# Chunked delta rule: three pairs of small matrix products issued alternately on the tensor engine, and the outputs of a tile computed half a step later

## The chip, the cores and the metric

One core of one Trainium2 chip runs the whole program as one launch. The metric is the device time of the program in microseconds (us), lower is better. An engine is named as the profile names it: PE (TensorE matrix products), PEld (its weight loads), DVE (VectorE), ACT (ScalarE), POOL (GpSimd). Each engine takes its instructions strictly in the order in which they are written; semaphores order the engines against each other.

## The reference, cut to what matters

The program is a two-layer decoder over x of 64 x 64 x 128. The change lies in one stage, the gated delta rule of the second layer, which the reference writes as a scan over 64 time steps:

```python
def step(carry, ins):
    s, mem = carry
    ...
    alpha = jnp.where(active > 0, alpha, jnp.ones_like(alpha))
    beta = beta * active
    s = s * alpha[..., None]
    pred = jnp.einsum('bhk,bhkv->bhv', kt, s)
    s = s + (beta * kt)[..., None] * (vt - pred)[:, :, None, :]
    out = jnp.einsum('bhk,bhkv->bhv', qt, s)
    return ((s, mem), out)
...
y = y * jax.lax.rsqrt(jnp.mean(y * y, axis=-1, keepdims=True) + EPS) * head_norm_w
y = y.reshape(B, T, H * dv)
gate = jax.nn.sigmoid(jax.nn.silu(x @ Wu1 + bu1) @ Wu2 + bu2)
y = x + y @ Wo * gate
```

All else (attention, cross attention, two mixtures, layer norms) is the same in both kernels.

## The kernel before, in words

The stage is `delta_rule`. The 64 sequences are cut into NT = 32 tiles of two sequences (TT = 128 tokens); a tile holds HB = 8 pairs of heads and sequences, and two heads share the 128 partitions, so that every small product is one of 64 x 64 on one half of the partitions. In place of the scan, a 64-step triangular system is solved by doubling: six levels (0 to 5) of decayed products of keys and queries (`level_one`), and beside them the inverse G and its transpose GT, grown level by level.

Two kinds of small product exist. `stay` takes its inputs from a half of the partitions and writes to the same half; `cross` writes to the other half. Each issues two products, one for each half, and an fp32 product is two matmul instructions in the trace. One block of eight `stay` (or eight `cross`) is 32 matmuls. Two of the blocks were already issued alternately, one `stay`, one `cross`: `z_and_level` (level l+1 and the step z of the inverse, 64 matmuls, from line 1895) and `g_and_gt` (the growth of G and of GT, 64 matmuls, from line 1916; at the top level, 4, only GT, 32 matmuls).

The work runs in a software pipeline by hand. `half(w_, x, y)` is one step of it: tile x goes through its levels, tile y = x + 1 is prepared (projections, gates, norms, values, `diagonal`, `level_zero`), and tile w_ = x - 1 is finished. `half` is written out for each engine, and the order of the calls in it is the order of that engine's queue. A tile is finished on PE by: `read_v` (GT times v, `cross`), `corrected` (the correction CT times RV, `cross`), `solve` (GT times W, `cross`), `outputs` (U times PT, `stay`), `head_norm`, `project_out`; each was a block of its own. `level_zero` (32 matmuls, `stay`) and `diagonal` were two more. Beside them ACT copies results out of PSUM (`keep_z`, `keep_rv`, `keep_u`, `square_y`) and does logarithms and exponentials; DVE scales, masks and adds (`scale`, `keep_ct`, `keep_pt`, `add_g`, `add_gt`, `subtract`, `strengths`, `normalise_y`); POOL scales the keys (`scale`), starts G and GT (`begin_g`, `begin_gt`), and does `push_logits`, `pair` and `floor_y`. After the last tile, `end` finishes tile 31.

PE's order in a half before: z_and_level 0, project_gates, read_v, g_and_gt 0, beta_sums, project_kq (first half), z_and_level 1, corrected, g_and_gt 1, count, project_kq (second half), z_and_level 2, solve, g_and_gt 2, outputs, norms, z_and_level 3, values, head_norm, g_and_gt 3, level_zero, diagonal, z_and_level 4, project_out, g_and_gt 4.

Of the kernel before, what the change touches and what calls it, by code (L numbers as in the profile page):

```python
# [14 lines left out]
ALU = mybir.AluOpType  # L15
# [1679 lines left out]
def delta_rule(k, s, w, hT, uT, gate, signs, yT):  # L1695
# [19 lines left out]
    log_q, q_eps = s.sb("log_q", [P, HB * T]), two("q_eps", [P, HB * T])  # L1715
# [3 lines left out]
    ylog, yinv = flat(RV), flat(W)  # L1719
# [56 lines left out]
    def in_turn(eng, front, half, end):  # L1776

        front(0)
        half(None, 0, 1)
        for tile in range(NT - 2):  # L1780
            half(tile, tile + 1, tile + 2)
        half(NT - 2, NT - 1, None)
        end(NT - 1)

    @block.tensor
    def _(pe):
# [67 lines left out]
        def norms(w_, y):  # L1854

            if w_ is not None:
                pe.wait_ge(u_kept, upto(w_))
# [23 lines left out]

        def level_zero(y):

            pe.wait_ge(kq_ready, upto(y))
            for n in range(HB):
                last = level_one(y, 0, n, F2)
            last.then_inc(level_ready[0], 1)
# [45 lines left out]
        def read_v(w_):  # L1933

            u = par(w_)
            pe.wait_ge(gt_kept[TOP], upto(w_))
            pe.wait_ge(out_kept, upto(w_))
            for n in range(HB):
                last = cross(lambda r: E0[r, wide(n)], lambda r: GT[u][r, n, :], lambda r: v[u][r, n % 2, n // 2, :])
            last.then_inc(rv_ready, 1)  # L1940

        def corrected(w_, y):
# [4 lines left out]
            pe.wait_ge(rv_kept, upto(w_))  # L1947
            pe.wait_ge(ct_kept[LEVELS - 1], upto(w_))
            for n in range(HB):
                last = cross(lambda r: E1[r, wide(n)], lambda r: CT[LEVELS - 1][r, n, :], lambda r: RV[r, n, :])  # L1950
            last.then_inc(crv_ready, 1)

        def solve(w_):

            u = par(w_)
            pe.wait_ge(w_ready, upto(w_))
            for n in range(HB):
                last = cross(lambda r: E0[r, wide(n)], lambda r: GT[u][r, n, :], lambda r: W[r, n, :])
            last.then_inc(u_ready, 1)

        def outputs(w_):

            u = par(w_)
            pe.wait_ge(u_kept, upto(w_))
            pe.wait_ge(pt_kept[LEVELS - 1], upto(w_))
            for n in range(HB):
                last = stay(lambda r: E1[r, wide(n)], lambda r: U[r, n, :], lambda r: PT[u][r, n, :])
            last.then_inc(y_ready, 1)

        def head_norm(w_, y):  # L1970

            u = par(w_)
            if y is not None:
                pe.wait_ge(logn_ready, upto(y))
            pe.wait_ge(floored, upto(w_))
# [10 lines left out]
        def front(y):  # L1986
# [4 lines left out]
            norms(None, y)  # L1991
            values(y)
            diagonal(y)
            level_zero(y)

        def end(w_):
            read_v(w_)
            corrected(w_, None)
            solve(w_)
            outputs(w_)  # L2000
            head_norm(w_, None)
            project_out(w_)

        def half(w_, x, y):
            z_and_level(w_, x, 0)
            if y is not None:
                project_gates(y, range(DP))
            if w_ is not None:
                read_v(w_)
            g_and_gt(w_, x, 0)  # L2010
            if y is not None:
                beta_sums(y)
                project_kq(y, (0, 1))
            z_and_level(w_, x, 1)
            if w_ is not None:
                corrected(w_, y)
            g_and_gt(w_, x, 1)
            if y is not None:
                count(y)
                project_kq(y, (2, 3))  # L2020
            z_and_level(w_, x, 2)
            if w_ is not None:
                solve(w_)
            g_and_gt(w_, x, 2)
            if w_ is not None:
                outputs(w_)
            if y is not None:
                norms(w_, y)
            z_and_level(w_, x, 3)
            if y is not None:  # L2030
                values(y)
            if w_ is not None:
                head_norm(w_, y)
            g_and_gt(w_, x, 3)
            if y is not None:
                level_zero(y)
                diagonal(y)
            z_and_level(w_, x, 4)
            if w_ is not None:
                project_out(w_)  # L2040
            g_and_gt(w_, x, 4)

        in_turn(pe, front, half, end)

    @block.scalar
    def _(act):
# [45 lines left out]
        def query_eps(w_, y):  # L2092
# [4 lines left out]
            if w_ is not None:  # L2097
                act.wait_ge(floored, upto(w_))
            act.activation(q_eps[par(y)][:, :], log_q[:, :], ACT.Square, scale=RMS_EPS ** 0.5, bias=q_floor[:, :]
# [16 lines left out]
        def square_y(w_):  # L2116
            act.wait_ge(y_ready, upto(w_))
            act.activation(ysq[:, :], E1, ACT.Square).then_inc(ysq_ready, 1)  # L2118
# [22 lines left out]
        def end(w_):  # L2141
            keep_rv(w_)
            keep_u(w_)
            square_y(w_)
            log_y(w_)
            inverse_y(w_)

        def half(w_, x, y):
            keep_z(x, 0)
            if y is not None:  # L2150
                stage(y)
            if w_ is not None:
                keep_rv(w_)
            keep_z(x, 1)
# [3 lines left out]
            keep_z(x, 2)  # L2158
            if w_ is not None:
                keep_u(w_)  # L2160
            if y is not None:
                square(y)
            if w_ is not None:
                square_y(w_)
            if y is not None:
                log_norms(y)
                log_queries(y)
                exp_beta(y)
            keep_z(x, 3)
            if y is not None:  # L2170
                exp_norms(y)
                query_eps(w_, y)
            if w_ is not None:
                log_y(w_)
                inverse_y(w_)
            keep_z(x, 4)

        in_turn(act, front, half, end)

    @block.gpsimd  # L2180
    def _(pool):
# [31 lines left out]
        def floor_y(w_):  # L2213
# [3 lines left out]
            pool.tensor_tensor(ysq[:, :], ysq[:, :], q_eps[par(w_)][:, :], ALU.add).then_inc(floored, 1)  # L2217
# [26 lines left out]
        def end(w_):  # L2244
            floor_y(w_)

        def half(w_, x, y):
            if y is not None:
                push_logits(y)
            scale(x, 1)  # L2250
            scale(x, 2)
            scale(x, 3)
            if w_ is not None:
                floor_y(w_)
            if y is not None:
                pair(y)
            scale(x, 4)
            if y is not None:
                begin_gt(w_, y)
                scale(y, 0)  # L2260
                begin_g(y)
# [3 lines left out]
        in_turn(pool, front, half, end)  # L2265

    @block.vector
    def _(dve):
# [75 lines left out]
        def diagonal(w_, y):  # L2344

            dve.wait_ge(diag_ready, upto(y))
            if w_ is not None:
                dve.wait_ge(y_ready, upto(w_))
# [84 lines left out]
        def front(y):  # L2433
# [7 lines left out]
            diagonal(None, y)  # L2441
# [3 lines left out]
            keep_pt(y, 0)  # L2445

        def end(w_):
            subtract(w_)
            normalise_y(w_)
            keep_out(w_)  # L2450

        def half(w_, x, y):
            keep_ct(x, 1)
            if y is not None:
                stage(y)
            decays(x, 1)
            keep_pt(x, 1)
            scale(x, 1)
            add_g(x, 0)
            if y is not None:  # L2460
                beta_logits(y)
                raise_logits(y)
# [698 lines left out]
```

## Time and profile before

| what | us |
|---|---|
| median of 3 runs | 2336.43 (2326.97 to 2350.22) |
| the profiled execution | 2313.16 |
| its span on the core | 2311.4 |
| PE busy in the span | 2062.0 (89%) |
| DVE busy | 1504.5 (65%) |
| ACT busy | 1108.9 (48%) |
| POOL busy | 686.6 (30%) |

The profile is one execution, and lies 1% below the median of the runs. A matmul's end is modelled in it, so the distance from the start of one block to the start of the next tells more than the duration of a block. The loop of the delta rule lies between 1059 and 1943 us of the span.

### The profile page before, as it was taken

To read this page: it belongs to the slowest core of one execution; us is meant where nothing else is said; L and a number is where in the kernel's file an instruction comes from. 1 tells how busy PE (TensorE), PEld (TensorE's weight loads), DVE (VectorE), ACT (ScalarE), POOL (GpSimd) and SP (SyncE) were. 2 spreads that over 40 slices of the span, in tenths; PEclk is the share of its full clock that TensorE was granted. 3 is DMA by queue.
4 is the path that set the end of the run, shared out by engine and by line. 5 is a ranking of instruction groups with operands and counts; after the bars stand their busy time and mean duration, and the time that the engine had idled before them with its cause. 6 is when DMAs were issued, how large, how long until landed. Compare 5 with 4: busy or idle time off the path is not lost. (4 is left out here: it accounts for less than half of the span.)

```text
span 2311.4 us, 90647 instructions
## 1 busy us (share of the span) xinstructions
PE 2062.0 (89%) x39947; PEld 1450.0 (63%) x39947; DVE 1504.5 (65%) x3187; ACT 1108.9 (48%) x1883; POOL 686.6 (30%) x731
## 2 busy tenths in 40 slices
PE   6999999789986779687999999999999996997998
PEld 3566666555643568126877888888787884445445
DVE  7878787456657744586777777777777774354214
ACT  2233334556667775673545444455454443244334
POOL 4656565022204100303333333333333332000000
PEclk7999999999998999898999999999999997997999
DMA  4000000000000000100000000000000001002001
GB/s 94 2 2 2 3 2 2 6 1 0 0 3 12 0 1 1 31 0 3 5 4 5 4 4 5 4 4 5 4 4 4 4 4 52 0 1 73 1 0 37
DMA packets 36492, 22.62 MB, mean 10 GB/s; under 512 B 16809, under 2 KB 32113, under 8 KB 36146
## 3 DMA queue, kind: packets, MB, share of 16 engines
q1 hardware_dynamic: 36146, 17.38, 3.0%
q8 instruction: 294, 4.82, 0.9%
q14 instruction: 52, 0.43, 0.1%
HBM read 15.28 MB, written 2.10 MB: 8 GB/s over the span
## 5 line engine op out<-in xcount | busy, mean ns | idle before, releaser
L1793 PEld LDWEIGHTS psum<-dr_kq,dr_kSq 64*64 64x64 f32 x6144 | 196.3, 134 | 64.1 <-issue 55.2
L1793 PE MATMUL psum<-dr_kq,dr_kSq 64*64 64x64 f32 x6144 | 222.2, 221 | 7.6 <-DVE dr_G L2404 2.9
L2105 ACT ACTIVATE dr_Y<-psum 128x256 f32<-128x256 f32 x160 | 62.9, 393 | 311.1 <-PE psum L1799 309.5
L1793 PE MATMUL psum<-dr_GT,dr_Y 64*64 64x32 f32 x5120 | 187.0, 221 | 12.7 <-issue 12.0
L1799 PE MATMUL psum<-dr_G,dr_CT 64*64 64x32 f32 x5120 | 184.1, 221 | 0.4 <-issue 0.2
L1793 PEld LDWEIGHTS psum<-dr_GT,dr_Y 64*64 64x64 f32 x5120 | 166.2, 135 | 19.0 <-issue 14.6
L1799 PEld LDWEIGHTS psum<-dr_G,dr_CT 64*64 64x64 f32 x5120 | 165.0, 134 | 1.0 <-issue 0.8
L2194 POOL TENSOR_TENSOR dr_kSq<-dr_kSq,dr_decay 128x256 f32<-128x256 f32 x128 | 99.4, 777 | 211.1 <-PE psum L1793 208.1
L1799 PE MATMUL psum<-dr_Y,dr_GT 64*64 64x32 f32 x4096 | 147.4, 219 | 14.6 <-issue 13.4
L1799 PEld LDWEIGHTS psum<-dr_Y,dr_GT 64*64 64x64 f32 x4096 | 135.3, 135 | 39.8 <-issue 37.8
L2395 DVE COPY_PREDICATED dr_PT<-dr_level_masks,psum 128x256 f32<-128x256 uint32 x192 | 102.7, 535 | 83.5 <-PE psum L1793 80.6
L2385 DVE TENSOR_TENSOR dr_CT<-psum,dr_minus_masks 128x256 f32<-128x256 f32 x192 | 78.5, 422 | 77.5 <-PE psum L1793 77.5
L2370 DVE TENSOR_TENSOR dr_kq<-dr_kq,dr_decay 128x512 f32<-128x512 f32 x128 | 114.5, 895 | 0.0
L537 ACT ACTIVATE attn_probsT<-psum 128x1024 f32<-128x1024 f32 x32 | 32.7, 1023 | 165.3 <-PE psum L383 165.3
L503 POOL TENSOR_TENSOR attn_q<-attn_by_cos,attn_by_sin 128x512 f32<-128x512 f32 x64 | 81.3, 1270 | 72.2 <-DVE attn_by_sin L450 71.0
L503 POOL TENSOR_TENSOR attn_k<-attn_by_cos,attn_by_sin 128x512 f32<-128x512 f32 x64 | 81.4, 1271 | 70.9 <-DVE attn_by_sin L450 70.3
L2217 POOL TENSOR_TENSOR dr_ysq<-dr_ysq,dr_q_eps 128x512 f32<-128x512 f32 x32 | 40.5, 1266 | 138.3 <-ACT dr_ysq L2118 138.3
L2413 DVE TENSOR_TENSOR dr_GT<-dr_GT,psum 128x256 f32<-128x256 f32 x160 | 66.3, 415 | 16.1 <-PE psum L1793 16.1
L3004 DVE COPY topk_outs<-psum 128x512 f32<-128x512 f32 x16 | 11.1, 692 | 99.9 <-PE psum L2894 99.9
L2202 POOL TENSOR_TENSOR dr_push<-dr_spikes_t,dr_alpha_spike 128x512 f32<-128x512 bf16 x32 | 37.9, 1185 | 118.1 <-ACT dr_spikes_t L2053 118.1
L2404 DVE TENSOR_TENSOR dr_G<-dr_G,psum 128x256 f32<-128x256 f32 x128 | 53.2, 416 | 27.1 <-PE psum L1799 25.9
L450 DVE SCALAR_TENSOR_TENSOR attn_by_cos<-psum,attn_qk_bias,attn_rope_q 128x512 f32<-128x512 f32 x64 | 47.8, 747 | 33.3 <-PE psum L356 32.2
(396 smaller groups left out, 5655.1 us busy)
## 6 DMA issues: line engine op xcount, KB each, us to landing
topk_w<-in_L_ffn_w_dram SPq DMA_DIRECT2D x16, 256.0 KB, 5.9
attn_w_x_rows<-in_x_dram SPq DMA_DIRECT2D x4, 512.0 KB, 6.0
out_dram<-store_rows SPq DMA_DIRECT2D x4, 512.0 KB, 4.0
dout_w<-in_L_attn_Wff_dram SPq DMA_DIRECT2D x3, 256.0 KB, 2.9
attn_w_rows<-in_L_attn_Wq_dram SPq DMA_DIRECT2D x1, 256.0 KB, 6.7
attn_w_rows<-in_L_attn_Wk_dram SPq DMA_DIRECT2D x1, 256.0 KB, 6.1
attn_w_rows<-in_L_attn_Wv_dram SPq DMA_DIRECT2D x1, 256.0 KB, 5.5
attn_w_rows<-in_L_attn_Wo_dram SPq DMA_DIRECT2D x1, 256.0 KB, 4.9
```

Source lines behind the costliest of these rows:

```text
L450: last = dve.scalar_tensor_tensor(dst[:, :].rearrange("p (n t) -> p n t", t=T), k.bank[2 * r + part][:, :].rearrange("p (n t) -> p n t", t=T),
L503: pool.tensor_tensor(qk[st % 2][g][:, hp, :], by_cos[st % 2][:, :], by_sin[st % 2][:, :], ALU.add).then_inc(roped, 1)
L1793: last = nc.tensor.matmul(out(r), lhsT(r), rhs(r), start=True, stop=True)
L1799: last = nc.tensor.matmul(out(HALVES[1 - j]), lhsT(r), rhs(r), start=True, stop=True)
L2105: act.activation(half_of(Y[l], l, 0), ZG[:, ZS].rearrange("p (m l) -> p m l", l=1 << l), ACT.Copy).then_inc(z_kept[l], 1)
L2194: pool.tensor_tensor(ks, ks, total.unsqueeze(2).to_broadcast([P, HB * (LR >> l), 1 << l]), ALU.mult).then_inc(kS_scaled[l], 1)
L2217: pool.tensor_tensor(ysq[:, :], ysq[:, :], q_eps[par(w_)][:, :], ALU.add).then_inc(floored, 1)
L2370: dve.tensor_tensor(right, right, pair[:, :, 0].unsqueeze(1).unsqueeze(3).to_broadcast([P, 2, HB * (LR >> l), L]), ALU.mult).then_inc(scal ...
L2385: dve.tensor_tensor(right4(CT[l], l), out[:, 0, :, :, :], minus.to_broadcast(shape), ALU.mult).then_inc(ct_kept[l], 1)
L2395: dve.copy_predicated(right4(PT[u], l), mask.bitcast(U32).to_broadcast(shape), out[:, 1, :, :, :]).then_inc(pt_kept[l], 1)
L2404: dve.tensor_tensor(left, left, ZG[:, RS].rearrange("p (m l) -> p m l", l=1 << l), ALU.add).then_inc(g_kept[l], 1)
L2413: dve.tensor_tensor(right, right, GTB[:, ZS].rearrange("p (m l) -> p m l", l=1 << l), ALU.add).then_inc(gt_kept[l], 1)
```

## The change

Three pairs of PE blocks become one block each, in which a `stay` and a `cross` alternate, as in `z_and_level`: `read_and_output(o, w_)` (the value read of tile w_ with the outputs of tile o = w_ - 1), `correct_and_level(w_, y)` (the correction of w_ with level zero of y), and `solve_and_gt(o, w_, x, y)` (the solve of w_ with the growth of GT at the top level of x). The outputs of a tile are now computed in the next half, so a half spans four tiles, `half(o, w_, x, y)`, and there is one more half; `end` is gone. The order of the calls changes on all four engines; `q_eps` gets a third buffer, and the logarithm of the head norm goes to `ysq` in place of `RV`. No instruction of computation is added or dropped.

```diff
-    log_q, q_eps = s.sb("log_q", [P, HB * T]), two("q_eps", [P, HB * T])
+    log_q, q_eps = s.sb("log_q", [P, HB * T]), [s.sb(f"q_eps{u}", [P, HB * T]) for u in range(3)]
...
-    ylog, yinv = flat(RV), flat(W)
+    ylog, yinv = ysq[:, :], flat(W)
...
+        def read_and_output(o, w_):
+
+            if w_ is not None:
+                pe.wait_ge(gt_kept[TOP], upto(w_))
+            if o is not None:
+                pe.wait_ge(u_kept, upto(o))
+                pe.wait_ge(pt_kept[LEVELS - 1], upto(o))
             for n in range(HB):
...
+                    last_v = cross(lambda r: E0[r, wide(n)], lambda r: g[r, n, :], lambda r: values_of[r, n % 2, n // 2, :])
+                if o is not None:
+                    last_y = stay(lambda r: E1[r, wide(n)], lambda r: U[r, n, :], lambda r: PT[par(o)][r, n, :])
...
+        def correct_and_level(w_, y):
...
+                pe.wait_ge(kq_ready, upto(y))
...
+                pe.wait_ge(rv_kept, upto(w_))
+                pe.wait_ge(ct_kept[LEVELS - 1], upto(w_))
             for n in range(HB):
...
+                    last_level = level_one(y, 0, n, F2)
...
+                    last = cross(lambda r: E1[r, wide(n)], lambda r: CT[LEVELS - 1][r, n, :], lambda r: RV[r, n, :])
...
+        def solve_and_gt(o, w_, x, y):
...
+                pe.wait_ge(w_ready, upto(w_))
...
+                pe.wait_ge(z_kept[TOP], upto(x))
+                pe.wait_ge(gt_kept[TOP - 1], upto(x))
...
```

The four queues of a full half after the change:

- PE: z_and_level 0, read_and_output, project_gates, g_and_gt 0, head_norm(o), z_and_level 1, project_kq (first half), count, g_and_gt 1, project_kq (second half), z_and_level 2, project_out(o), beta_sums, g_and_gt 2, norms, z_and_level 3, g_and_gt 3, correct_and_level, z_and_level 4, values, solve_and_gt, diagonal.
- ACT: stage(y), keep_z 0, square_y(o), keep_rv(w_), log_y(o), inverse_y(o), keep_z 1, gate(y), keep_kSq(y), keep_z 2, square(y), exp_beta(y), keep_z 3, log_norms, log_queries, exp_norms, keep_z 4, query_eps(y), keep_u(w_).
- POOL: push_logits(y), floor_y(o), scale 1, scale 2, scale 3, pair(y), scale 4, begin_g(y), scale(y, 0), begin_gt(y).
- DVE: scale 1, diagonal, keep_pt 0 and 1, keep_ct 1, add_g 0, stage(y), decays 1, raise_logits(y), add_gt 0, keep_pt 2, scale 2, keep_ct 2, add_g 1, decays 2, normalise_y(o), add_gt 1, gates(y), keep_pt 3, keep_out(o), scale 3, keep_ct 3, add_g 2, beta_logits(y), weigh(y), add_gt 2, decays 3, keep_pt 4, scale 4, keep_ct 4, add_g 3, add_gt 3, strengths(y), subtract(w_), scale(y, 0), keep_pt 5, keep_ct(y, 0), keep_ct 5, add_gt 4, decays(y, 0), keep_v(y).

## Rows read from the trace of the kernel before

**Rows 1.** The page: busy time by engine, and PE clock in 40 slices.

```profile
PE 2062.0 (89%) x39947; PEld 1450.0 (63%) x39947; DVE 1504.5 (65%) x3187; ACT 1108.9 (48%) x1883; POOL 686.6 (30%) x731
...
PEclk7999999999998999898999999999999997997999
```

**Rows 2.** Busy time by stretch: length, then PE, PEld, DVE, ACT, POOL, clock, DMA.

```profile
1103.75:1918.42 814.67, 775.38 (x25456) 657.12 (x25460) 611.90 (x1616) 398.32 (x655) 299.31 (x299) 1.00 0.02 4
```

**Rows 3.** Source line L2118: count, ns min/median/max, first and last start.

```profile
L2118 ACT ACTIVATE dr_ysq<-psum x31: 597/597/597, 1103.7 to 1918.4; 128x512 f32<-128x512 f32 x31
```

**Rows 4.** PE's waits, 1100 to 1930: line, releaser, us in total, times, longest.

```profile
PE psum L1793 <- issue: 17.4, 24, 1.2
PE psum L1799 <- issue: 16.8, 24, 1.2
PE psum L1793 <- DVE dr_G L2404: 2.9, 3, 1.6
```

**Rows 5.** PE's timeline from 1501.8: start, us, then [idle before].

```profile
1501.86 1.07 PE L1799 MATMUL psum<-dr_RV,dr_CT 64*64 64x64 f32 x30
1502.72 0.25 PE L1793 MATMUL psum<-dr_GT,dr_Y 64*64 64x32 f32 x2
...
1503.43 0.25 PE L1793 MATMUL psum<-dr_GT,dr_Y 64*64 64x32 f32 x2 [0.23 <-issue]
...
1506.93 0.24 PE L1799 MATMUL psum<-dr_G,dr_CT 64*64 64x32 f32 x1
...
1510.68 0.32 PE L1793 MATMUL psum<-dr_PT,dr_U 64*64 64x64 f32 x2 [0.72 <-issue]
1510.94 1.08 PE L1860 MATMUL psum<-dr_head_sum,dr_sq 128*128 128x32 f32 x8
...
1512.89 0.27 PE L1793 MATMUL psum<-dr_kq,dr_kSq 64*64 64x64 f32 x2
...
1513.96 1.08 PE L1871 MATMUL psum<-dr_wv,dr_h 128*64 128x256 f32 x8
1514.98 1.13 PE L1976 MATMUL psum<-dr_ysq,dr_head_mean 128*128 128x512 f32 x2
1516.03 0.25 PE L1799 MATMUL psum<-dr_Y,dr_GT 64*64 64x32 f32 x2
...
1517.00 1.13 PE L1793 MATMUL psum<-dr_kq,dr_kSq 64*64 64x64 f32 x32
```

**Rows 6.** PE's timeline, another run of pauses.

```profile
1611.31 0.25 PE L1799 MATMUL psum<-dr_Y,dr_GT 64*64 64x32 f32 x2 [0.45 <-issue]
...
1618.69 0.53 PE L1860 MATMUL psum<-dr_head_sum,dr_sq 128*128 128x32 f32 x4 [0.45 <-issue]
```

**Rows 7.** DMA, 1103.75 to 1918.42: queue, packets, MB, share.

```profile
q8 instruction: 202, 3.31, 1.7%
```

**Rows 8.** DMA, 1501 to 1511, in 40 slices of 0.25 us: busy tenths.

```profile
DMA  2000000000000020000000000000300000000000
```

**Rows 9.** DVE, by shape, 1100 to 1930, and its timeline around `strengths`.

```profile
L2370 DVE TENSOR_TENSOR dr_kq<-dr_kq,dr_decay 128x512 f32<-128x512 f32 x122 | 109.3, 896 | 0.0
...
L2395 DVE COPY_PREDICATED dr_PT<-dr_level_masks,psum 128x256 f32<-128x256 uint32 x183 | 97.6, 533 | 79.4 <-PE psum L1793 76.5
...
1515.67 0.69 DVE L2318 TENSOR_SCALAR dr_length<-dr_norm 64x4 f32<-64x4 f32 x4
...
1517.76 0.42 DVE L2404 TENSOR_TENSOR dr_G<-dr_G,psum 128x256 f32<-128x256 f32 x1
```

**Rows 10.** The page: ACT's `keep_z` and POOL's `floor_y`; xcount, busy, mean ns, idle before.

```profile
L2105 ACT ACTIVATE dr_Y<-psum 128x256 f32<-128x256 f32 x160 | 62.9, 393 | 311.1 <-PE psum L1799 309.5
...
L2217 POOL TENSOR_TENSOR dr_ysq<-dr_ysq,dr_q_eps 128x512 f32<-128x512 f32 x32 | 40.5, 1266 | 138.3 <-ACT dr_ysq L2118 138.3
```

**Rows 11.** The last tile after the loop: ACT's and DVE's timeline.

```profile
1928.67 0.60 ACT L2110 ACTIVATE dr_RV<-psum 128x512 f32<-128x512 f32 x1 [3.66 <-PE psum L1799]
...
1942.61 0.29 DVE L2431 TENSOR_TENSOR delta_hT<-psum,ctx_rows 128x128 f32<-128x128 f32 x1 [2.17 <-PE psum L1982]
```

More of the change, by code:

```diff
@@ L1953, in solve @@
[L1953 to L1968, printed above, removed]
@@ L1990, in front, with half @@
             count(y)
-            norms(None, y)
+            norms(None, None, y)
             values(y)
             diagonal(y)
[L1994 to L2005, printed above, removed]
+            correct_and_level(None, y)
+        def half(o, w_, x, y):
+            if x is not None:
+                z_and_level(w_, x, 0)
+            read_and_output(o, w_)
@@ L2021, in half @@
[L2021 to L2029, printed above, removed]
+            if x is not None:
+                g_and_gt(w_, x, 2)
+            if y is not None:
+                norms(o, w_, y)
+            if x is not None:
+                z_and_level(w_, x, 3)
+                g_and_gt(w_, x, 3)
@@ L2444, in front, with half @@
             scale(y, 0)
[L2445 to L2453, printed above, removed]
+        def half(o, w_, x, y):
+            if x is not None:
+                scale(x, 1)
+                diagonal(o, x)
+                keep_pt(x, 0)
+                keep_pt(x, 1)
+                keep_ct(x, 1)
+                add_g(x, 0)
             if y is not None:
                 stage(y)
[L2456 to L2459, printed above, removed]
+            if x is not None:
+                decays(x, 1)
+            if y is not None:
+                raise_logits(y)
+            if x is not None:
+                add_gt(x, 0)
+                keep_pt(x, 2)
+                scale(x, 2)
+                keep_ct(x, 2)
+                add_g(x, 1)
+                decays(x, 2)
+            if o is not None:
+                normalise_y(o)
+            if x is not None:
+                add_gt(x, 1)
+            if y is not None:
+                gates(y)
+            if x is not None:
+                keep_pt(x, 3)
+            if o is not None:
+                keep_out(o)
+            if x is not None:
+                scale(x, 3)
+                keep_ct(x, 3)
+                add_g(x, 2)
@@ L2460, in half @@
             if y is not None:
                 beta_logits(y)
-                raise_logits(y)
-            add_gt(x, 0)
-            keep_pt(x, 2)
-            scale(x, 2)
+                weigh(y)
+            if x is not None:
+                add_gt(x, 2)
+                decays(x, 3)
+                keep_pt(x, 4)
+                scale(x, 4)
+                keep_ct(x, 4)
+                add_g(x, 3)
+                add_gt(x, 3)
+            if y is not None:
+                strengths(y)
@@ L2505, in _ @@
-        in_turn(dve, front, half, end)
+            if x is not None:
+                keep_ct(x, 5)
+                add_gt(x, 4)
+            if y is not None:
+                decays(y, 0)
+                keep_v(y)
+        in_turn(front, half)
 def delta_output(k, yT):
```

225 lines of the change are left out of this document (105 added, 120 removed).

## The prediction

> **What bounds the kernel now.** I read the page first, then the timeline of one tile on every engine, then the waits of PE, then the DMA queues. PE is busy 89% of the span and 95% of the delta loop: 775.38 of 814.67 us, at a granted clock of 1.00, that is 2.4 GHz [rows 1, 2]. The squares of the outputs come once a tile; the 31 of them from 1103.7 to 1918.4 enclose 30 periods, so a tile takes 814.67 / 30 = 27.16 us [rows 2, 3]. DVE, next in the list, works 611.90 / 30 = 20.4 us of it [rows 2]. In the timeline one PE block starts where the one before ends; PE waits for data almost nowhere: of its idle time by releaser, 34.2 us are "issue" and 2.9 us a DVE result [rows 4]. "Issue" is time in which the profile shows nothing to wait for.
>
> What the pauses are can be seen in the DMA queue of instructions. It has 202 packets and 3.31 MB in those 30 tiles, 6.73 packets of 16.4 KB a tile [rows 7]. PE runs 850 matmuls a tile (count of the calls), so one packet stands for 126 matmuls with their weight loads. The timeline's pauses stand just so far apart: 1503.43, 1506.93, 1510.68, and 1611.31, then 1618.69 two packets on [rows 5, 6]; and in the first of these stretches the packets themselves run 3.5 us apart (slices 0, 14 and 28 of 0.25 us) [rows 8]. So when 126 matmuls are done sooner than the next packet can be had, PE stands. The price of a packet in such runs is (3.50 + 3.75 + 7.38) / 4 = 3.66 us. Over the loop a packet comes each 27.16 / 6.73 = 4.03 us: PE is not far above the pace of its instructions. I read the stage as bound by PE's blocks where they are slow, and by instruction packets where they are dense.
>
> The Trainium skill, page "Runtime: NRT & Kernel Launch", section "Instruction fetch mechanics", says that the queue is refilled in blocks of 16 KiB while the engine works, and that crossing a block is mostly hidden. The size agrees with the trace (16.4 KB a packet); "mostly hidden" doesn't in the dense stretches (0.72 us idle at 1510.68). By the page the change would keep all it takes off PE; that is the first rival.
>
> **The change, part by part.**
>
> *The three pairs.* A block of one kind, 32 matmuls, has its first 30 started in 0.86 us (RV, CT at 1501.86, next block at 1502.72), so about 0.92 us whole. A mixed block of 64 takes 0.97 us (1516.03 to 1517.00), and 1.07 with the change to another shape (1512.89 to 1513.96) [rows 5]. A second kind of product between the first costs next to nothing. Three pairs (correction with level zero, solve with GT, value read with outputs) make three blocks of 0.97 out of six of 0.92 to 0.95, 2.7 us less a tile, and two shape changes fewer, 0.1 each: 2.9 us. PE's blocks then sum to 22.6 us instead of 25.5 (27.16 less 39.3 / 30 = 1.3 idle, less some 0.3 of modelled ends that count as busy) [rows 2].
>
> *Instruction packets.* No matmul goes, so 6.73 packets a tile stay, and their floor is 6.73 x 3.66 = 24.6 us, above the 22.6 us of work. To see what gets through I put the blocks in a row with their starts' distances (mixed 0.98, norms 1.95, values 1.02, head norm 1.05, gates, key projections, output projection and diagonal about 1.08 each, beta 0.68, count 0.24), cut the row every 126 matmuls over four tiles (27 pieces) and filled each piece under 3.66 us up to it. Before: 25.5 us of work and 1.6 us of fill a tile, 27.1, against 27.16 measured; the reading holds. After: 22.6 us and 3.5 us of fill, 26.1. The fill doubles because the dense blocks now stand together: g_and_gt 3 and the correction with level zero pass 126 matmuls in 1.97 us, a fill of 1.7 us, while the piece over g_and_gt 2 and norms has 3.8 us or more and saves nothing. Of 2.9 us, 1.05 are kept. With 3.4 us a packet, the least that the 0.25 us slices allow, the same sum gives a saving of 1.3. I take 1.15 us a tile, nearer to 3.66, which more rows carry.
>
> *Waits of the new order.* (a) z_and_level 3 is followed at once by g_and_gt 3, which needs ACT's copy of z (0.39 us [rows 10]) with its signals, 0.5 us; before, values and the head norm lay between (1513.96 to 1516.03). Behind it on PE wait the whole last third, and DVE's add_g 3. (b) solve_and_gt waits for `subtract`, which is queued on DVE behind `strengths`, 2.09 us of small instructions (1515.67 to 1517.76 [rows 9]). From the end of z_and_level 3 DVE does keep_pt 4 (0.34), scale 4 (0.9), keep_ct 4, add_g 3 and add_gt 3 (1.0), strengths 2.1, subtract 0.6: 4.9 us, PE 0.5 + 4 x 1.0 = 4.5: a wait of 0.4. (c) The next z_and_level 0 needs keep_ct 5: another scale (1.2), two keep_ct, one keep_pt (1.0), 7.2 us in all from z_and_level 3, against 7.0 on PE: 0.2. (d) POOL does floor_y (1.27 [rows 10]) before scale 1 in the new order; the squares come at 2.1 us of the half, floor_y ends at 4.1, scale 1 at 5.3, where PE wants it at 5.2: 0.1. Together 1.2 us, if nothing else stopped PE: 23.8 us, still below the packets' 24.6. A packet asked for before a wait arrives during it, so (a) to (c), which all lie in the stretch with the largest fills, cost nothing by themselves; if the cover fails they cost up to 0.5 + 0.4 + 0.2 + 0.1 = 1.2 us a tile. I take nothing.
>
> *DVE, ACT, POOL elsewhere.* The same instructions in another order; DVE's 20.4 us in 26.0 leave room, and so does ACT's 398.32 / 30 = 13.3 us. The third q_eps buffer and the other place of the logarithm cost no instruction. Free.
>
> *Front and end.* The outputs of tile 31 come one half later. Before, from the value read's copy (1928.67) to the last keep_out (1942.61) 13.9 us of a plain chain [rows 11]. After, the squares, floor, head norm, logarithm, exponential, product and projection of tile 30 stand before the correction of tile 31 on PE, 5 to 6 us. The first halves lose a diagonal and a mask, 1 us. Sum: 4 us more; bounds 0 and 8.
>
> *Sum.* 31 x 1.15 = 36 us less, 4 us more: 32 us less. From the profiled execution's 2313.2 us this makes 2281; it lies 1% below the median of the runs, 2336.4, and I forecast on the median: 2304 us. Its own range: 0.8 to 1.6 us a tile, and 0 to 8 at the end, 2288 to 2315.
>
> **Rivals.**
>
> *The packets don't bind (0.15).* If the pace of packets can rise when PE drains them faster, PE's work with its waits sets the tile: 23.8, and 0.4 for pauses left, 24.2 us. 31 x 2.95 = 91 less, 4 more: 2249 us. For it: packets at the loop's mean come 4.03 us apart and the queue moves 1.7% of its share [rows 7]. Against: the pauses stand exactly one packet apart, at 3.5 to 3.75 us [rows 5]. This is where the skill's "mostly hidden" would end.
>
> *The packets take it all (0.2).* The stretch's mean is 4.03 us a packet; at 3.9 in the dense stretches the floor is 26.2, and with 0.6 for slow pieces the tile takes 26.8. 31 x 0.35 = 11 less, 4 more: 2329 us, no change to be told. For it: dense blocks now follow each other, and the packet is asked for only after the crossing. Against: the triples' 3.66.
>
> *Slower: pauses and waits add (0.12).* The place is the last third of a half. PE reaches the end of z_and_level 3 after 584 matmuls, 4.6 packets, 17.7 us. The rest is 266 matmuls, 6.1 us of work, with two fills of 1.7 each, 9.5 us; if a fill falls before the matmul that DVE waits for, and (a) to (c) come on top instead of beneath, 10.6. A tile then takes 28.3: 31 x 1.14 = 35 more, 4 more: 2375 us. It decides from 9.5 us on, for then 17.7 + 9.5 passes 27.16. For it: DVE's queue from z_and_level 3 on has no gap (7.2 us). Against: a pause for a packet is also time for DVE.
>
> **How the numbers follow.** My forecast has 0.53, the rivals 0.15, 0.2 and 0.12. About 1% (23 us) is what a measurement of this kernel can tell from no change. Faster by over 1% (under 2313): all of the first rival and 0.42 of the forecast's 0.53, 0.57. Within 1%: the remaining 0.11 and the second rival, 0.31. Slower by over 1% (over 2360): 0.12. The range leaves out the slower rival and the far half of the first: 2258 to 2336.
>
> **What would show it.** Right: the tile at 26.0 us by the squares of the outputs; PE busy down by 2.9 us a tile, PE's "issue" idle up from 1.3 to some 3 us; packets still 6.73 a tile, now 3.86 us apart; pauses in g_and_gt 3 or the correction block. The first rival: packets under 3.4 us apart, "issue" not up. The slower one: PE's waits name DVE's `subtract` (dr_W) and ACT's dr_Y with whole us a tile, and the tile passes 27.2. Wrong altogether, if a mixed block of a value read and outputs takes clearly more than 1.0 us.

## The result, and the profile after

| | before | after |
|---|---|---|
| median of 16 runs, us | 2330.6 (2322.37 to 2350.22) | 2353.04 (2343.62 to 2359.35) |
| the profiled execution, its span | 2313.16, 2311.4 | 2357.34, 2355.6 |

The change makes the kernel slower by 0.9%: the ratio is 1.0092, with a 95% interval from 1.0073 to 1.0111. That lies outside the range of the prediction, 2258 to 2336 us, and on the other side of no change; by size it belongs to the case within 1%, which had 0.31. The two profiled executions differ by 44 us, the medians by 22: the one of before lies 17 us under its median and 7.7 of the 44 us lie outside the delta rule, in code that didn't change. What follows compares lengths of a tile, each from the one profiled execution of a kernel. Where the 17 us of before lie can't be told from one trace; were they all in the loop, its tile would be 0.6 us longer in the median execution than in the profile. So comparisons with the tile of before are less certain than those among the later kernels, and the medians are given beside them.

Page of the kernel after, busy time by engine and granted clock in 40 slices, as in [rows 1]:

```profile
PE 2022.5 (86%) x39885; PEld 1400.4 (59%) x39947; DVE 1576.0 (67%) x3187; ACT 1101.8 (47%) x1883; POOL 659.9 (28%) x731
...
PEclk7999999999998999988999999999999996997999
```

PE has 39.5 us less work than before and DVE 71.5 us more, though both kernels give DVE the same 3187 instructions. That second number is the first sign of what went wrong.

For the length of a tile, the squares of the outputs from 1150 to 1900 us, before, after and in the first experiment (with one wait put back, below):

```profile
L2118 ACT ACTIVATE dr_ysq<-psum x28: 597/597/597, 1157.0 to 1889.8; 128x512 f32<-128x512 f32 x28
```

```profile
L2127 ACT ACTIVATE dr_ysq<-psum x27: 597/597/599, 1152.8 to 1880.2; 128x512 f32<-128x512 f32 x27
```

```profile
L2127 ACT ACTIVATE dr_ysq<-psum x29: 597/597/597, 1151.3 to 1899.4; 128x512 f32<-128x512 f32 x29
```

A tile takes (1889.8 - 1157.0) / 27 = 27.14 us before, (1880.2 - 1152.8) / 26 = 27.98 after, and (1899.4 - 1151.3) / 28 = 26.72 with the wait put back. Every "tile" below is worked out like this, and a total is put on a tile by 750 us over its length.

Busy time from 1150 to 1900 us (length, PE, PEld, DVE, ACT, POOL, granted clock, DMA), before, then after:

```profile
1150.00:1900.00 750.00, 716.08 (x23466) 605.79 (x23458) 565.23 (x1493) 374.31 (x612) 277.71 (x277) 1.00 0.02 4
```

```profile
1150.00:1900.00 750.00, 657.94 (x22875) 535.97 (x22874) 612.77 (x1450) 354.89 (x590) 243.44 (x269) 0.97 0.02 4
```

On a tile: PE 25.9 us before and 24.5 after, so the alternation did take work off PE. DVE 20.5 before and 22.9 after. The mean granted clock fell from 1.00 to 0.97. Of DVE's additional 2.4 us, 2.1 are found in three groups by shape (same window). Before:

```profile
L2359 DVE TENSOR_TENSOR dr_decay<-dr_alpha 128x256 f32<-128x256 f32 x27 | 11.2, 415 | 0.0
L2332 DVE COPY dr_crossed<-dr_length 64x8 f32<-64x8 f32 x56 | 9.3, 166 | 1.3
L2333 DVE COPY dr_crossed<-dr_strength 64x8 f32<-64x8 f32 x56 | 8.9, 160 | 0.0
```

After:

```profile
L2339 DVE COPY dr_crossed<-dr_strength 64x8 f32<-64x8 f32 x53 | 32.0, 604 | 0.0
L2365 DVE TENSOR_TENSOR dr_decay<-dr_alpha 128x256 f32<-128x256 f32 x27 | 29.3, 1085 | 0.0
L2338 DVE COPY dr_crossed<-dr_length 64x8 f32<-64x8 f32 x53 | 25.0, 471 | 1.3
```

The copies of 64 x 8 elements, among the smallest work that DVE does, went from 0.16 and 0.17 us to 0.60 and 0.47 in the mean, and one product of 128 x 256 from 0.42 to 1.09. Neither has changed in itself; what has changed is what POOL does at the time. The timeline of one tile of the kernel after (start, us, engine), DVE at the end of `strengths`:

```profile
1512.97 0.17 DVE L2338 COPY dr_crossed<-dr_length 64x8 f32<-64x8 f32 x1
1513.05 1.03 DVE L2339 COPY dr_crossed<-dr_strength 64x8 f32<-64x8 f32 x1
1514.10 0.79 DVE L2338 COPY dr_crossed<-dr_length 64x8 f32<-64x8 f32 x1
1514.80 0.16 DVE L2339 COPY dr_crossed<-dr_strength 64x8 f32<-64x8 f32 x1
1514.99 0.69 DVE L2426 TENSOR_TENSOR dr_W<-psum,dr_v 128x512 f32<-128x512 f32 x1
```

POOL at the same time:

```profile
1513.02 1.04 POOL L2231 TENSOR_TENSOR dr_G<-dr_eye,dr_strength 128x512 f32<-128x512 f32 x1 [3.27 <-DVE dr_strength L2335]
1514.02 0.84 POOL L2201 TENSOR_TENSOR dr_kSq<-dr_kSq,dr_alpha 128x256 f32<-128x256 f32 x1
```

And PE:

```profile
1515.89 0.32 PE L1790 MATMUL psum<-dr_GT,dr_Y 64*64 64x32 f32 x2 [2.26 <-issue]
```

Read the starts and ends. POOL's `begin_g` starts at 1513.02 and ends at 1514.06; DVE's copy that starts at 1513.05 ends at 1514.08. POOL's next instruction ends at 1514.86; DVE's next copy, from 1514.10, ends at 1514.89. These two DVE copies from SBUF to SBUF each end with the POOL instruction that they meet, 0.02 and 0.03 us after it, though one POOL instruction took 1.04 us and the other 0.84: the copies don't run at some lower speed, they stand until POOL is done. The two meetings cost 0.87 + 0.62 = 1.5 us, and `strengths` takes from 1511.40 to 1514.99, 3.6 us, instead of the 2.1 of [rows 9]. Behind it in DVE's queue stands `subtract`, and for `subtract` waits the solve on PE, which is idle for 2.26 us. (The page of the kernel calls this wait "issue"; `subtract` ends at 1515.68 and the solve starts 0.2 us later, so part of what is named "issue" is this wait.)

The Trainium skill, page "SBUF — State Buffer", section "Who interferes with whom", says that VectorE and GpSimd share a pair of SBUF ports under an exclusive lock for a whole instruction, that a VectorE copy can need it, and that the loser is fully blocked. The ends 0.02 and 0.03 us apart agree.

POOL waits in `begin_g` for `strong`, raised by the product just before the four small copies, and in `begin_gt` for `turned`, raised by the last of them. Before the change `begin_gt` came first in POOL's queue, so that POOL stood until DVE's copies were through. With `begin_g` first it starts exactly beside them.

The clock is the second part. Windows of the same tile, columns as above:

```profile
1513.00:1515.89 2.89, 0.64 (x6) 0.17 (x3) 2.84 (x6) 1.34 (x3) 1.84 (x2) 0.98 0.00 0
1515.89:1518.00 2.11, 2.11 (x65) 1.99 (x66) 1.53 (x5) 0.07 (x1) 0.00 (x0) 0.50 0.03 8
```

After PE's wait the granted clock is 0.50, that is 1.2 GHz. The block of 64 matmuls starts at 1515.89 and what follows it at 1517.81: 1.92 us, where [rows 5] have 0.97. It doesn't happen in every tile. The mean of 0.97 over 750 us bounds what it costs: 0.03 x 750 = 22 us, 0.8 a tile, if PE had been at work all the time. The first experiment below gives 0.5.

PE's largest waits from 1150 to 1900 (us, times, longest), after:

```profile
PE psum L1790 <- issue: 47.7, 52, 2.3
PE psum L1796 <- issue: 22.3, 28, 1.8
PE psum L1796 <- ACT dr_Y L2112: 14.6, 27, 0.5
```

Before these were 15.9 and 15.2 us of "issue" in the same window, and no ACT row.

### The profile page after: what moved, and what is told of

It is laid out like the page before. It is cut to its first block and busy times, and to the rows that moved or that the text cites. A ratio compares the mean times of both kernels' runs of the same rounds, so it can differ in the third digit from the quotient of the medians.

```text
span 2355.6 us, 90619 instructions
## 1 busy us (share of the span) xinstructions
PE 2022.5 (86%) x39885; PEld 1400.4 (59%) x39947; DVE 1576.0 (67%) x3187; ACT 1101.8 (47%) x1883; POOL 659.9 (28%) x731
## 5 line engine op out<-in xcount | busy, mean ns | idle before, releaser
L1790 PEld LDWEIGHTS psum<-dr_kq,dr_kSq 64*64 64x64 f32 x6144 | 204.3, 137 | 108.4 <-issue 80.0
L1790 PE MATMUL psum<-dr_kq,dr_kSq 64*64 64x64 f32 x6144 | 229.6, 225 | 24.8 <-issue 16.7
L1790 PE MATMUL psum<-dr_GT,dr_Y 64*64 64x32 f32 x5120 | 194.5, 224 | 32.2 <-issue 29.9
L1790 PEld LDWEIGHTS psum<-dr_GT,dr_Y 64*64 64x64 f32 x5120 | 173.4, 138 | 49.4 <-issue 49.0
L1796 PE MATMUL psum<-dr_G,dr_CT 64*64 64x32 f32 x5120 | 190.9, 224 | 12.5 <-issue 12.5
L2201 POOL TENSOR_TENSOR dr_kSq<-dr_kSq,dr_decay 128x256 f32<-128x256 f32 x128 | 86.4, 675 | 339.5 <-PE psum L1790 339.5
L1796 PEld LDWEIGHTS psum<-dr_G,dr_CT 64*64 64x64 f32 x5120 | 170.8, 138 | 13.9 <-issue 13.8
L1796 PE MATMUL psum<-dr_Y,dr_GT 64*64 64x32 f32 x4096 | 152.7, 221 | 26.9 <-ACT dr_Y L2112 17.8
L2376 DVE TENSOR_TENSOR dr_kq<-dr_kq,dr_decay 128x512 f32<-128x512 f32 x128 | 124.4, 972 | 14.2 <-PE psum L1790 12.5
L510 POOL TENSOR_TENSOR attn_probs<-attn_exp,attn_row_inv 128x1024 f32<-128x1024 f32 x32 | 60.9, 1904 | 28.3 <-DVE attn_row_inv L474 24.8
L3053 ACT ACTIVATE topk_hid<-psum 128x1024 f32<-128x1024 f32 x32 | 32.8, 1024 | 75.2 <-PE psum L2893 75.2
```

What stands on the lines that cost most here:

```text
L510: pool.tensor_tensor(rows_of(probs[:, :, :]), rows_of(expd[:, :, :]), inv[:, :].unsqueeze(2).to_broadcast([P, AH, T]), ALU.mult).then_inc( ...
L1790: last = nc.tensor.matmul(out(r), lhsT(r), rhs(r), start=True, stop=True)
L1796: last = nc.tensor.matmul(out(HALVES[1 - j]), lhsT(r), rhs(r), start=True, stop=True)
L2201: pool.tensor_tensor(ks, ks, total.unsqueeze(2).to_broadcast([P, HB * (LR >> l), 1 << l]), ALU.mult).then_inc(kS_scaled[l], 1)
L2376: dve.tensor_tensor(right, right, pair[:, :, 0].unsqueeze(1).unsqueeze(3).to_broadcast([P, 2, HB * (LR >> l), L]), ALU.mult).then_inc(scal ...
```

## The experiments

The theories at the start: (P) POOL beside DVE's copies makes the solve late; (Q) the order of DVE alone does, `strengths` before `subtract`; (R) instruction packets of PE take what the alternation gives; (S) the new waits (ACT's z among them) cost what the prediction had taken as hidden. Ratios are against the kernel before, with 95% intervals; each "tile" is from one profiled execution. In the expectations Theory A is (P), and Theory B is (R) or (S).

**One wait put back.** The kernel after, with `begin_g` held until DVE's copies are done.

```diff
         def begin_g(y):
...
-            pool.wait_ge(strong, upto(y))
+            pool.wait_ge(turned, upto(y))
```

> The changed kernel, with POOL's begin_g waiting for the end of strengths (turned) and not for the strength alone (strong). Theory A (POOL's product and DVE's small copies hold each other, and DVE's queue from strengths to keep_ct 5 sets the tile): the copies into crossed fall from a mean of 524 ns to about 165 ns, DVE's busy time per tile from 22.8 us to 21.3 us, the tile from 27.9 us to 26.1 to 26.5 us, and the total to 2295 to 2310 us, about 1% under the kernel before. Theory B (the new order of the waits or the packets set the tile whatever the copies take): the copies fall too, but the tile stays at 27.5 us or more and the total at 2345 to 2355 us. Theory C (the copies are slow for a reason that isn't POOL): the copies stay near 524 ns and nothing moves.

Measured: 2322.19 us, ratio 0.9969 (0.9937 to 1.0001); tile 26.72. The copies, one row of the source line in the kernel after and one here (count, ns min/median/max):

```profile
L2339 DVE COPY dr_crossed<-dr_strength x64: 156/162/1033, 1060.2 to 1929.5; 64x8 f32<-64x8 f32 x64
```

```profile
L2339 DVE COPY dr_crossed<-dr_strength x64: 156/159/165, 1060.7 to 1893.1; 64x8 f32<-64x8 f32 x64
```

The longest of these copies is 0.165 us again: they no longer meet POOL. The row of the window and PE's waits here:

```profile
1150.00:1900.00 750.00, 675.27 (x23945) 552.26 (x23937) 611.00 (x1515) 370.25 (x618) 266.69 (x280) 1.00 0.02 4
```

```profile
PE psum L1790 <- issue: 28.2, 48, 1.6
PE psum L1796 <- issue: 26.2, 36, 1.6
PE psum L1796 <- ACT dr_Y L2112: 15.2, 28, 0.5
```

"Issue" falls from 70.0 / 26.8 = 2.6 us a tile to 54.4 / 28.1 = 1.9, and the clock is back at 1.00. All idle time of PE falls from (750 - 657.94) / 26.8 = 3.4 us a tile to (750 - 675.27) / 28.1 = 2.7, and its busy time, for the same matmuls, from 24.5 to 24.1, which leaves the clock as the reason. These two, 0.8 and 0.5, are the 1.26 us a tile between this kernel and the one after. By the medians the wait is worth less, 1.0092 - 0.9969 = 0.0123, or 29 us in 31 tiles, 0.9 a tile. Either way one wait takes away the whole loss: with the collision the change adds 0.84 us to a tile, without it it takes off 0.42 by the traces. By the medians the gain isn't clear of noise (the interval ends at 1.0001), and it is less than was expected, 26.1 to 26.5 us a tile and 2295 to 2310 in all.

**`subtract` ahead of `strengths`**, first with POOL as in the kernel after, then with the wait put back as well.

```diff
-            if y is not None:
-                strengths(y)
             if w_ is not None:
                 subtract(w_)
             if y is not None:
+                strengths(y)
+            if y is not None:
                 scale(y, 0)
```

> The changed kernel, with DVE's subtract(w_) ahead of strengths(y); POOL as in the changed kernel. Theory A, in which the tile is set by the end of DVE's queue (keep_ct 5 before the next z_and_level 0) as well as by subtract: the copies stay at 500 ns or more, PE no longer idles 1 to 2 us before the solve block, but 1.5 us of the copies still stand before keep_ct 5, so that the tile gets only 0.6 to 1.3 us shorter, 26.6 to 27.3 us, and the total is 2315 to 2340 us. Theory A', in which the wait for subtract is all of it: 26.0 to 26.3 us, as with the copies mended. Theory B: 27.5 us or more.

> The changed kernel with both edits: begin_g waits for turned, and subtract stands ahead of strengths. If instruction packets then set the tile, as the prediction's sum has it, this is no faster than begin_g's wait alone by more than 0.2 us a tile: 26.0 to 26.3 us, PE's idle time named issue about 3 us a tile, and no half-speed stretches of PE's clock in the loop. If packets don't bind, the second edit takes another 0.4 us or more: 25.6 us or less.

Measured: 2361.72 us (1.0135, 1.0087 to 1.0182), tile 28.27; and with the wait 2338.77 us (1.0056, 1.0024 to 1.0089), tile 27.36. With (P) alone 26.6 to 27.3 us was expected, and 26.0 to 26.3 with the wait; both were missed, and 28.27 falls by its size to Theory B, which the first experiment speaks against. Moving the work that PE waits for to the front brought nothing. With the wait put back it is clearly slower, 1.0056 against 0.9969; without it 0.3 us a tile longer, while the intervals of the ratios (1.0087 to 1.0182 here, 1.0073 to 1.0111 for the kernel after) overlap. DVE's timeline in the first of the two:

```profile
1518.20 0.69 DVE L2426 TENSOR_TENSOR dr_W<-psum,dr_v 128x512 f32<-128x512 f32 x1 [1.56 <-PE psum L1796]
...
1520.45 1.03 DVE L2339 COPY dr_crossed<-dr_strength 64x8 f32<-64x8 f32 x1
1521.49 0.79 DVE L2338 COPY dr_crossed<-dr_length 64x8 f32<-64x8 f32 x1
...
1523.33 0.76 DVE L2391 TENSOR_TENSOR dr_CT<-psum,dr_minus_masks 128x256 f32<-128x256 f32 x2
```

and PE's waits there:

```profile
PE psum L1790 <- DVE dr_CT L2391: 19.6, 23, 1.4
```

`subtract` now stands 1.56 us for PE's correction in this tile, 15.0 us in 26 tiles (0.58 in the mean; 15.5 in 27 with the wait put back), and the rest of the queue stands behind it; `strengths` had filled that time. All that DVE has left of the half comes later by as much, and in the first of the two PE waits for `keep_ct` at the start of the next half. (In the second no such row is among PE's largest.) So (Q), the order on DVE, is not the cause; the order of the change is the better one. In both orders the wait on POOL is worth about the same: 28.27 - 27.36 = 0.91 here, 1.26 above.

**The collision in the kernel before.** Only POOL's order at the end of a half is changed; PE, DVE and ACT are those of before.

```diff
             if y is not None:
-                begin_gt(w_, y)
-                scale(y, 0)
                 begin_g(y)
+                scale(y, 0)
+                begin_gt(w_, y)
```

> The kernel before, with POOL's last three calls in the order of the changed kernel (begin_g, scale(y, 0), begin_gt), so that begin_g runs beside strengths. Theory A: the copies into crossed go from 163 ns to about 520 ns in the mean, 1.0 us the longest; strengths then ends 1.5 us later, before add_g 3 and add_gt 3. Between z_and_level 3 and 4 PE has 3 us of other work there, so the tile grows by 0.3 to 1.0 us, the total by 10 to 30 us. Theory C: the copies stay at 163 ns.

Measured: 2360.68 us, 1.0153 (1.0096 to 1.021); tile 28.17, 1.0 us more than before, at the upper end of what was expected (0.3 to 1.0). Its copies, and PE's first wait:

```profile
L2333 DVE COPY dr_crossed<-dr_strength x64: 156/163/1033, 1064.6 to 1934.2; 64x8 f32<-64x8 f32 x64
```

```profile
PE psum L1793 <- DVE dr_G L2404: 17.8, 24, 0.8
```

The same 1.033 us as in the kernel after, and PE waits for the `add_g` that is queued behind `strengths`, a wait of 2.9 us in all before [rows 4]. With no alternation and no new order on the other engines, POOL's order alone makes the kernel about as slow as the whole change did (1.0092, 1.0073 to 1.0111). This and the first experiment show (P) from both sides: the collision goes with its one wait and comes with POOL's order.

**80 more instructions for PE.** The kernel before, with four waits that are already met behind each of the 20 slow matmuls of a tile. They cost the blocks no time that shows: the starts of the value block and the next are 1.01 us apart in most tiles of both kernels, and in the same way the gates and the output projection are unchanged at 1.09, the two products of the norms at 0.91 and 1.03. What is left for them to act through are the instruction packets.

```diff
+                for _ in range(4):
+                    pe.wait_ge(consts, 2)
```

> The kernel before, with 80 more waits a tile in PE's queue, on a semaphore that is long set; they stand in fours behind the slow matmuls of gates, key projections, norms, values and output projection, where PE still has 0.1 to 0.25 us of work at hand for each. They make the instruction stream longer by 80 / 256 of a packet and leave the work as it is. If packets set part of the time: 7.06 packets a tile instead of 6.75, and 0.4 to 0.55 us a tile more (the prediction's sum over pieces gives 27.6 instead of 27.1 us), 12 to 17 us in all. If packets don't bind: 7.06 packets and less than 0.1 us a tile. If a wait costs more than its cover, PE's distance between the blocks gates, norms and values themselves grows; that can be read from the timeline.

Measured: 2345.84 us, 1.0079 (1.0046 to 1.0111); tile 27.92. The packet rows from 1150 to 1900, before and here:

```profile
q8 instruction: 186, 3.05, 1.7%
```

```profile
q8 instruction: 185, 3.03, 1.7%
```

That is 186 / 27.6 = 6.73 a tile before and 185 / 26.9 = 6.89 here, half of the additional packets that were expected (7.06); why it is half is open. By 3.66 us a packet the 0.16 are 0.6 us a tile, 18 us in 31 tiles; the medians differ by 17 to 18. The largest rows of PE's idle time are again "issue":

```profile
PE psum L1799 <- issue: 22.3, 37, 1.6
PE psum L1793 <- issue: 19.4, 24, 1.2
```

They go from 31.1 / 27.6 = 1.1 us a tile to 41.7 / 26.9 = 1.6. So (R) is borne out as far as these runs go: PE pays for the instructions that it is sent, though they do nothing. That it pays at the packets follows from the blocks being unchanged, and isn't seen by itself. "Mostly hidden", as the Trainium skill has it (page "Runtime: NRT & Kernel Launch", section "Instruction fetch mechanics"), doesn't hold here: 80 more instructions a tile cost 0.8% of the kernel.

**Alternation undone.** The first experiment's kernel, with the merged blocks issued one kind after the other.

```diff
             for n in range(HB):
...
                     last_v = cross(...)
+            for n in range(HB):
                 if o is not None:
                     last_y = stay(...)
```

(the same in the other two blocks)

> The changed kernel with begin_g waiting for turned, and with the three merged blocks issued in the same places but first the whole of one kind and then the whole of the other, not alternately. PE's work grows by 2.7 us a tile. If packets take most of what alternation brings (the prediction's sum over pieces: 26.9 against 26.05), the tile grows by 0.6 to 1.1 us to 27.3 to 27.8 us. If PE's work sets the tile: 2.5 us or more, 29.2 us. If DVE sets it: under 0.4 us.

Measured: 2335.91 us, 1.0022 (0.9991 to 1.0053); tile 27.23, 0.5 us more than the first experiment where 0.6 to 1.1 was expected for packets and 2.5 or more for PE's work. Its window and waits:

```profile
1150.00:1900.00 750.00, 712.06 (x23415) 596.17 (x23415) 583.52 (x1483) 365.78 (x607) 264.18 (x276) 1.00 0.02 4
```

```profile
PE psum L1790 <- issue: 10.5, 20, 1.0
PE psum L1796 <- issue: 9.3, 15, 1.3
```

PE's busy time goes from 675.27 / 28.1 = 24.1 us a tile to 712.06 / 27.5 = 25.9, while "issue" goes from 1.9 to 0.7. Of the 1.8 us that the alternation takes off PE (2.7 by the starts of blocks) the tile gets 27.23 - 26.72 = 0.5. The other 1.3 come back as idle time, 1.2 of it "issue". Most of that is put down to the packets by the argument above; a trace doesn't tell a wait for a packet from another wait named "issue".

**DVE relieved.** The first experiment, with `decays(y, 0)` moved ahead of `keep_pt(x, 4)`, away from POOL's `begin_gt`.

> The changed kernel with begin_g waiting for turned, and with DVE's decays(y, 0) moved from beside POOL's begin_gt (where it took 1.15 us instead of 0.41) into DVE's gap ahead of keep_pt 4, where POOL is idle. If DVE's held instructions still set the tile after the first mending: decays back to 0.41 us, DVE's busy time 21.7 to 21.0 us, the tile 26.7 to 26.2 us, the total 10 to 18 us under e1_turned. If PE and its packets set it now: decays back, but the tile within 0.15 us of 26.7.

Measured: 2321.2 us, 0.9969 (0.9944 to 0.9993), the same ratio as in the first experiment; tile 26.94 (at a mean clock of 0.99), no better than 26.72 and nearer to "within 0.15 us" than to the gain. The product itself is cured:

```profile
L2365 DVE TENSOR_TENSOR dr_decay<-dr_alpha 128x256 f32<-128x256 f32 x28 | 11.7, 417 | 0.0
```

0.67 us a tile less on DVE bring nothing. Though POOL held this product back, it was off the path: not every collision costs. It also answers whether DVE sets the tile once the copies are free: it doesn't.

**Blocks spread.** The kernel of the last experiment, with the values between z_and_level 3 and g_and_gt 3 and the diagonal ahead of the solve, so that a slow block stands between dense ones.

> e6_decays, with PE's values moved between z_and_level 3 and g_and_gt 3 and diagonal between z_and_level 4 and solve_and_gt: the slow blocks then cover the two copies of z by ACT, and the dense blocks stand less close. Expected by the packets' sum: PE no longer waits for ACT's dr_Y (0.54 us a tile), the fill falls by 0.3 to 0.5 us, the tile is 25.7 to 26.2 us, the total 2290 to 2310 us, 1% under the kernel before. If the waits for ACT lay beneath pauses anyway: the same as e6_decays within 0.15 us a tile.

Measured: 2335.68 us, 1.0031 (1.0005 to 1.0058); tile 27.25, where 25.7 to 26.2 was expected. The wait for ACT's z is gone, but two others have come:

```profile
PE psum L1790 <- issue: 31.4, 39, 1.9
PE psum L1796 <- issue: 30.6, 36, 2.1
PE psum L1790 <- DVE dr_CT L2392: 6.3, 14, 1.0
PE psum L1790 <- DVE dr_W L2427: 4.8, 9, 0.9
```

"Issue" is 2.3 us a tile, more than the 1.9 of the first experiment. The expectation's 0.3 to 0.5 us less of fill had not been worked out for this order; the prediction's sum over pieces of 126 matmuls, done afterwards, gives 0.2 to 0.3 us more, which has the sign of what was measured. Nor need the order alone be to blame, for this execution has the mean clock of the kernel after:

```profile
1150.00:1900.00 750.00, 671.67 (x23328) 547.75 (x23327) 572.72 (x1479) 363.54 (x604) 265.73 (x275) 0.97 0.02 4
```

How much of the loss is the new waits, the packets or the clock wasn't tried apart.

**The second product of the norms moved.** The first experiment's kernel with this product behind z_and_level 3, and then with `decays(y, 0)` moved too.

```diff
+        def query_norms(y):
             nc.tensor.matmul(F1[:, :], w.head_sum[:, :], sq[:, 1, :], ...)
...
                 z_and_level(w_, x, 3)
+            if y is not None:
+                query_norms(y)
+            if x is not None:
                 g_and_gt(w_, x, 3)
```

> The changed kernel with begin_g waiting for turned, and with the second product of norms (the norms of the queries, 1.05 us) moved behind z_and_level 3, where it covers ACT's copy of z and parts two dense blocks; the norms of the keys, on which strengths hangs, stay ahead. The prediction's sum over pieces gives 0.3 us a tile less fill, and the wait for ACT's dr_Y (0.54 us a tile) has a cover: if both count, the tile is 25.9 to 26.4 us and the total 2295 to 2312 us, under both kernels. If the wait lay beneath the pauses of the packets, only the 0.3 is left: 26.3 to 26.6 us. If the order in the last third is set by DVE, nothing moves, or it gets slower as with values moved there (27.3 us).

> e9_split_norms and DVE's decays(y, 0) moved to its gap, as in e6_decays. Where PE and its packets set the tile, the same as e9_split_norms within 0.15 us a tile; where DVE has become the bound because PE reaches z_and_level 3 earlier, 0.3 to 0.7 us a tile less.

Measured: 2314.64 us, 0.9954 (0.9925 to 0.9984), and 2316.05 us, 0.9949 (0.9921 to 0.9977). These are the best kernels found: half a per cent under before, and no ACT row among PE's waits. That is short of the 25.9 to 26.4 us a tile that was expected with both gains. Their profiled tiles are 27.03 and 26.74 us, not shorter than the first experiment's 26.72; but both profiled executions are the slowest of their twelve, 2327.14 and 2332.24 us, and the first of them lost some clock:

```profile
1150.00:1900.00 750.00, 682.47 (x23613) 556.69 (x23614) 608.11 (x1505) 371.01 (x613) 263.82 (x278) 0.98 0.02 4
```

Moving `decays(y, 0)` on top makes the profiled tile 0.29 us shorter, with the clock back at 1.00, and leaves the median where it was; so nothing shows DVE to have become the bound. The ratios' intervals overlap with the first experiment's, so whether removing the wait brought anything is not settled.

## Why the prediction was wrong

The step that failed is "DVE, ACT, POOL elsewhere: the same instructions in another order ... Free". It priced each instruction by its duration before, and that duration was a property of the old order. "Free" also left out the wait that this makes for PE. `strengths` was taken at 2.1 us from [rows 9] and takes 3.6 when `begin_g` and `scale(y, 0)` run beside it. It could have been seen in the kernel and the lists of calls: POOL's `begin_g`, now the first of its last three calls, waits for `strong`, and four DVE copies come between `strong` and `turned`.

The tile, by the prediction's own terms:

- *PE's work.* Mixed blocks of 0.97 us: right (in the kernel after, value read and outputs start at 1520.5 and end by 1521.5). PE busy down 1.4 us with the clock's loss in it, 1.8 in the unpaired comparison, against 2.9 by starts of blocks.
- *Packets.* "6.73 stay", "the fill doubles" to 3.5 and "of 2.9 us, 1.05 are kept": right in kind, too hopeful in size. The packets stay within a few hundredths (6.75), "issue" grows from 1.1 us a tile to 1.9 with the collision taken away, and 0.5 us are kept of the three pairs.
- *Sum.* 26.1 us predicted, 26.0 taken; 26.72 with the collision taken away. The difference is about as large as wait (a), but the runs without (a) don't show shorter tiles. The forecast's own range is also added up too narrowly: 31 x 0.8 less and 8 more makes 2320 us, not 2315. Even without the collision the forecast misses: the first experiment's 2322.19 us lies outside both.
- *Wait (a)*, ACT's z at 0.5 us "taken as nothing": PE waits 0.54 us in every tile of the kernel after. So it is not covered by packets, as PE stands there in plain sight. What its removal gives, 0.9954 against 0.9969, couldn't be told from the medians.
- *Wait (b)*, `subtract` behind `strengths`, 0.4 us and hidden: the place was right, the size by the same sum is 0.4 + 1.5, and 2.26 us of idle time were seen in the tile shown. Nor was it foreseen that PE could come out of that wait at half the clock. Waits (c) and (d), 0.2 and 0.1 us, have no row among PE's waits in the kernel after, except one of 0.4 us in all for POOL's `floor_y`; but a wait named "issue" can hide them, as it hid (b).
- *Ends.* 4 us more were predicted. From the first copy of the input to the last output the delta rule takes 898.8 us before, 935.3 after and 897.9 with the wait put back. Less 31 tiles of 0.84 more or 0.42 less, the ends cost 10.5 to 12 us, past the bound of 8. Where they go was not tried apart, but the granted clock in the first tiles is one place to look. From 1059 to 1103.75 us, before and in the first experiment:

```profile
1059.00:1103.75 44.75, 37.09 (x1312) 32.15 (x1310) 33.46 (x80) 19.09 (x29) 15.42 (x16) 1.00 0.02 4
```

```profile
1059.00:1103.75 44.75, 39.04 (x1008) 31.44 (x1010) 30.76 (x80) 15.72 (x26) 15.59 (x15) 0.78 0.01 3
```

A clock of 0.78 over 44.75 us is at most 9.8 us lost. The ends are why a tile of 0.42 us less gives the first experiment so little.

- *Rivals.* "Slower: pauses and waits add" had 0.12 and gave 28.3 us a tile; 27.98 came. Its end was near, its mechanism was not: it added the waits (a) to (c) to packets, and the main cost was an instruction held by another engine's. That nearness is luck. "The packets don't bind" speaks of 24.2 us; the 80 waits, and 0.5 us kept of 1.8, are against it. "The packets take it all" had 0.2, with 26.8 us a tile and 2329 us, no change to be told. Once the collision is taken away it comes nearest of all, the forecast included: 26.72 us and 2322.19, a ratio whose interval touches 1.

By the traces, of the +0.84 us a tile, order and pairs give -0.42 and the collision +1.26; by the medians the collision is 0.9. The -0.42 is the least certain of these, as it rests on the one execution of before.

## What to carry to other kernels

Before pricing a new order of DVE and POOL, list what each will run beside the other: a duration read from the old trace holds only for the old neighbours, and a tiny SBUF copy may take as long as the POOL instruction that it meets. A wait for an earlier semaphore isn't always a gain; here a later one, at no cost that shows, was worth 0.9 to 1.3 us in 28. After the change, look first for groups whose count stayed and whose mean rose.

## What the runs showed that I had not expected

- Copies of 64 x 8 elements from SBUF to SBUF took 1.03 us instead of 0.16 beside a POOL instruction, but `subtract` (one input in PSUM) took 0.69 us beside `begin_g`, the same 0.69 as in the kernel after, where POOL stood idle. In the first experiment:

```profile
1519.64 0.69 DVE L2426 TENSOR_TENSOR dr_W<-psum,dr_v 128x512 f32<-128x512 f32 x1
```

```profile
1519.68 1.04 POOL L2231 TENSOR_TENSOR dr_G<-dr_eye,dr_strength 128x512 f32<-128x512 f32 x1 [3.79 <-DVE dr_crossed L2339]
```

- 80 waits a tile that are already met cost 0.8% of the whole kernel, as expected, but with 0.16 more packets a tile, not 0.31.
- An idle time of PE of 2.26 us was followed by blocks at a granted clock of 0.50, so that the next block alone took another 0.95 us. The length of the idle time doesn't decide it: after 1.59 us in the first experiment, and after 2.21 us (before 1771.89) with `subtract` ahead of `strengths`, the windows stay at 1.00.

```profile
1520.30:1522.00 1.70, 1.70 (x60) 1.12 (x53) 1.70 (x5) 1.26 (x3) 1.69 (x2) 1.00 0.04 10
```

```profile
1771.89:1774.00 2.11, 2.10 (x71) 1.52 (x75) 2.06 (x4) 1.18 (x3) 1.52 (x2) 1.00 0.03 8
```
